# Two state matmuls of a recurrent attention loop over 128 partitions in place of 64: three become two, ten become six

## The chip, the cores and the metric

The kernel runs on one core of a Trainium2 chip. The metric is the device time of one execution in microseconds. Beside the plain runs there is one execution under the hardware profiler, and every row below comes from it.

## The reference, cut to what matters

A small network of two layers: cross attention, a quantised feed-forward, then a recurrent attention with a state of 64 values, and a mixture of experts. The change touches only the recurrent part. It has 256 steps that follow one another, for a batch of 4. In the reference, one step is

```python
def step(carry, tgt):
    s, c, alpha = carry
    f = conv(alpha, conv_w)
    e = einsum('a,bta->bt', va, tanh(enc_proj + (s @ Wa_s.T)[:, None, :] + einsum('bft,af->bta', f, Wa_f) + ba))
    alpha_new = softmax(where(mask, e, -1e30), axis=1)
    g = einsum('bt,btd->bd', alpha_new, hbatch)
    y = tanh(g @ L_gy_w.T + L_gy_b + s @ L_sy.T) @ L_yy_w.T + L_yy_b
    rec = tgt @ L_ys.T + s @ L_ss.T + g @ L_gs_w.T + L_gs_b
    ig, fg, cg, og = split(rec, 4, axis=1)
    c_next = sig(fg) * c + sig(ig) * tanh(cg)
    s_next = sig(og) * tanh(c_next)
```

The state `s` (64 values for each of 4 sequences) enters two products in the loop: `s @ Wa_s.T` inside the tanh, and `s @ L_ss.T` inside the gates.

## The kernel before, in words

Three stages follow one another. Attention and the first feed-forward take the first 445 us. Then comes the recurrent loop, 128 turns of a hardware loop with two steps in each (`l` is the step), and last the mixture of experts. In the loop each engine has its own instruction queue, worked off in order, and the engines are tied together by semaphores alone.

Float32 numbers are multiplied in 16-bit pieces. The state is kept as `sh` (its fp16 rounding) and `sl` (the rest), each of 64 partitions by 4 columns. `was2` holds the high and the low half of `Wa_s` (64 partitions, two blocks of 128 columns), `lss3` three bf16 parts of `L_ss` (64 partitions, three blocks of 256 columns).

One step of the loop, from the end of the state's update:

- VectorE (DVE) writes `sh` (L783), `s2` (L784, float32) and `sl` (L786).
- TensorE (PE) adds the state into `bank[0]`, where the encoder part already lies: three matmuls at L1200 with 64 contraction rows and 128 moving columns each, high weights times `sh`, low weights times `sh`, high weights times `sl`. The first waits for `sh`, the third for `sl`; the last raises `pre_done`.
- PE then forms `s @ L_ss.T` in `bank[6]`: ten matmuls at L1206, again 64 rows, 4 moving columns each, five for either half of the gates. The last raises `sp_done`.
- `keep_busy(n)` (L1188) is a matmul of n moving columns over 128 partitions into a bank that nobody reads. One of 384 columns follows the ten.
- ScalarE (ACT) waits for `pre_done` and takes the tanh twice: L955 in fp16 (`th_hi`), L956 in float32 (`th`).
- DVE, in its own order: L743 waits for `sp_done` and adds the input's part of the gates (`rs`); L746 waits for L956 and writes `th_lo`, the rest of the tanh; L749 takes a maximum.
- PE, in its own order: eight small matmuls at L1214 on `th_hi`, two at L1219, a `keep_busy(512)`, and L1222 on `th_lo`, which raises `et_done`.
- ACT takes the exponentials (L960, L961) once `et_done` and the maximum are there. Softmax sums, gates, the next cell and the next `sh` follow from them. Two `keep_busy(512)` are the last matmuls ahead of the next step's L1200.

Before the loop, DVE splits the weights (`in_parts` and `in_halves`, L705 to L713) while TensorE is in the second feed-forward half, and POOL (GpSimd) clears `sh` and `sl`. TensorE waits before the loop until `part_ready` is 5.

Of the kernel before, what the change touches and what calls it, by code (L numbers as in the profile page):

```python
# [7 lines left out]
ALU = mybir.AluOpType  # L8
ACT = mybir.ActivationFunctionType
F32 = mybir.dt.float32  # L10
F16 = mybir.dt.float16
BF16 = mybir.dt.bfloat16
# [4 lines left out]
P = 128  # L17
B, S, H = 4, 256, 512
# [9 lines left out]
J = 64  # L28
KW = 101
FCH = 10  # L30
TH = T // 2
# [46 lines left out]
def build(nc, a, out):  # L78
    with ExitStack() as ctx:
        def sb(name, shape, dt=F32):  # L80
            return ctx.enter_context(nc.sbuf_tensor(name, shape, dt))

        def sem(name):
            return ctx.enter_context(nc.semaphore(name))
# [34 lines left out]
        lss3 = sb("lss3", [J, 3, 256], BF16)  # L119
        lsyT = sb("lsyT", [J, J])  # L120
        wasT = sb("wasT", [J, P])
        was2 = sb("was2", [J, 2, P], F16)
# [42 lines left out]
        gat = sb("gat", [P, 8])  # L165
        rs = sb("rs", [P, 8])
        ahn = sb("ahn", [P, 8])
        sh = sb("sh", [J, B], F16)
        sl = sb("sl", [J, B], F16)
        qv = krep[:, 0, :, :].rearrange("p b t -> p (b t)").rearrange("p (i b t) -> p i b t", i=2, b=B)  # L170
        tfi = sb("tfi", [J, 8])
        xs = sb("xs", [J, 2, 12])
        ab = sb("ab", [J, 8])
        tc_sb = sb("tc_sb", [J, B])
        s2 = sb("s2", [J, 2, B])
# [30 lines left out]
        bank = [ctx.enter_context(nc.psum_tensor(f"bank{i}", [P, 512], F32)) for i in range(8)]  # L206
# [62 lines left out]
        s = {n: sem("s_" + n) for n in names}  # L269
# [115 lines left out]
        def _(pool):  # L385
# [78 lines left out]

            nc.gpsimd.memset(xs[:], 0.0)
            nc.gpsimd.memset(s2[:], 0.0).then_inc(s["s_ready"], 1)
            nc.gpsimd.memset(sh[:], 0.0).then_inc(s["sh_ready"], 1)
            nc.gpsimd.memset(sl[:], 0.0).then_inc(s["sl_ready"], 1)
            nc.gpsimd.memset(vah[:], 0.0)
            nc.gpsimd.memset(vae[:], 0.0).then_inc(s["pchain"], 1)  # L470
            pool.wait_ge(s["pchain"], 3)
# [68 lines left out]
        def _(dve):  # L540
            chain = [0]

            def link(ins):

                chain[0] += 1
                ins.then_inc(s["chain"], 1)
                dve.wait_ge(s["chain"], chain[0])
# [28 lines left out]
            def dequantise(n):  # L576

                product, integers, _, _ = weight_slice(n)
                dve.wait_ge(w_in[min(n, 8)], 16)
                dve.wait_ge(w_sc[n % 4], 16 * (n // 4 + 1))  # L580
                nc.vector.scalar_tensor_tensor(product, integers, WSCALE, product, ALU.mult, ALU.mult).then_inc(s["product_ready"], 1)
# [121 lines left out]
            def in_halves(dst, src):  # L703

                link(nc.vector.tensor_copy(dst[:, 0], src))  # L705
                nc.vector.tensor_tensor(dst[:, 1], src, dst[:, 0], ALU.subtract).then_inc(s["part_ready"], 1)

            def in_parts(dst, src):

                for j in range(2):  # L710
                    link(nc.vector.tensor_copy(dst[:, j], src))
                    link(nc.vector.tensor_tensor(src, src, dst[:, j], ALU.subtract))
                nc.vector.tensor_copy(dst[:, 2], src).then_inc(s["part_ready"], 1)  # L713
# [10 lines left out]
            dve.wait_ge(s["scale_ready"], 1)  # L724
            in_parts(lss3[:], lssT[:])
            in_halves(was2[:], wasT[:])
            dve.wait_ge(s["setup_v"], 1)
            in_halves(vae2[:], vae[:].rearrange("p h b -> p (h b)"))
            swiglu(IT0, IT0, False, context_parts())
# [4 lines left out]
            def by_half(ap):  # L734
                return ap.rearrange("p (o b) -> p o b", o=2)


            with dve.Fori(0, S // 2) as i:
                for par in range(2):
                    l = i * 2 + par  # L740

                    dve.wait_ge(s["sp_done"], l + 1)
                    nc.vector.tensor_tensor(rs[:].unsqueeze(1), bank[6][:, 0:8].unsqueeze(1), rin2[:, bass.ds(i, 1), par, :], ALU.add)  # L743

                    dve.wait_ge(s["th_full"], l + 1)
                    nc.vector.tensor_tensor(th_lo, th, th_hi, ALU.subtract).then_inc(s["th_lo_ready"], 1)  # L746

                    dve.wait_ge(s["eb_done"], l + 1)
                    nc.vector.tensor_reduce(nmx[:], bank[2][:, 0:T], AX.X, ALU.max, negate=True).then_inc(s["mx_ready"], 1)  # L749

                    dve.wait_ge(s["ex_ready"], l + 1)
                    nc.vector.tensor_tensor(el[:], ex[:, par, :], eh[:], ALU.subtract).then_inc(s["el_ready"], 1)  # L752

                    dve.wait_ge(s["sum_done"], l + 1)
                    nc.vector.reciprocal(rinv[:, par, :], bank[5][:, 8:12]).then_inc(s["rinv_ready"], 1)  # L755

                    norm = rinv[:, par:par + 1, :].broadcast_to([P, 2, B])
                    dve.wait_ge(s["rinv_ready"], l + 1)
                    dve.wait_ge(s["hg_done"], l + 1)
                    nc.vector.tensor_tensor(by_half(g1[:]), by_half(bank[4][:, 0:8]), norm, ALU.mult).then_inc(s["prod_ready"], 1)  # L760

                    def spread(h):

                        return nc.vector.tensor_tensor(qv[:, h, :, :], inv[:].unsqueeze(1).broadcast_to([P, B, TH]),  # L764
                                                       ahn[:, 4 * h:4 * h + 4].unsqueeze(2).broadcast_to([P, B, TH]), ALU.mult)


                    dve.wait_ge(s["ah_done"], l + 1)
                    nc.vector.tensor_tensor(by_half(ahn[:]), by_half(bank[7][:, 0:8]), norm, ALU.mult).then_inc(s["ahn_ready"], 1)
                    dve.wait_ge(s["prod_ready"], l + 1)  # L770
                    nc.vector.tensor_tensor(gat[:], g1[:], rs[:], ALU.add).then_inc(s["g_ready"], 1)  # L771
                    dve.wait_ge(s["ahn_ready"], l + 1)
                    spread(0).then_inc(s["q0_ready"], 1)
                    dve.wait_ge(s["kept"], l + 1)
                    spread(1).then_inc(s["q1_ready"], 1)

                    dve.wait_ge(s["tg_ready"], l + 1)
                    nc.vector.scalar_tensor_tensor(ab[:], tfi[:], 1.0, xs[:, par, 0:8], ALU.add, ALU.mult).then_inc(s["ab_ready"], 1)
                    dve.wait_ge(s["ab_ready"], l + 1)
                    nc.vector.scalar_tensor_tensor(xs[:, 1 - par, 0:4], ab[:, 0:4], 0.5, ab[:, 4:8], ALU.mult, ALU.add).then_inc(s["c_ready"], 1)  # L780

                    dve.wait_ge(s["tc_ready"], l + 1)
                    nc.vector.scalar_tensor_tensor(sh[:], xs[:, par, 8:12], 1.0, tc_sb[:], ALU.add, ALU.mult).then_inc(s["sh_ready"], 1)  # L783
                    nc.vector.scalar_tensor_tensor(s2[:, 1 - par, :], xs[:, par, 8:12], 1.0, tc_sb[:], ALU.add, ALU.mult).then_inc(s["s_ready"], 1)  # L784
                    dve.wait_ge(s["s_ready"], l + 2)
                    nc.vector.tensor_tensor(sl[:], s2[:, 1 - par, :], sh[:], ALU.subtract).then_inc(s["sl_ready"], 1)  # L786

# [211 lines left out]
        def _(pe):  # L1001
            mm = nc.tensor.matmul
# [166 lines left out]
            pe.wait_ge(s["setup_v"], 1)  # L1169
            pe.wait_ge(s["mask_ready"], 1)  # L1170
            pe.wait_ge(s["rin_ready"], 2 * B)
            pe.wait_ge(s["part_ready"], 5)
            pe.wait_ge(s["identb_ready"], 1)

            def masks():
# [17 lines left out]
            with pe.Fori(0, S // 2) as i:  # L1193
                for par in range(2):
                    l = i * 2 + par

                    state_part = [(0, sh), (1, sh), (0, sl)]
                    for j, st in state_part:
                        pe.wait_ge(s["sl_ready" if st is sl else "sh_ready"], l + 1)
                        last = mm(bank[0][:, 0:P], was2[:, j, :], st[:].unsqueeze(2).broadcast_to([J, B, TH]),  # L1200
                                  start=False, stop=(st is sl), skip_group_check=True)
                    last.then_inc(s["pre_done"], 1)

                    for gp in range(2):
                        for j, st in ((0, sh), (1, sh), (2, sh), (0, sl), (1, sl)):
                            last = mm(bank[6][:, 4 * gp:4 * gp + 4], lss3[:, j, gp * P:(gp + 1) * P], st[:],  # L1206
                                      start=(j == 0 and st is sh), stop=(j == 1 and st is sl))
                    last.then_inc(s["sp_done"], 1)

                    keep_busy(384)  # L1210
# [1 line left out]
                    for b in range(B):  # L1212
                        for h in range(2):
                            last = mm(bank[2][b * TH:(b + 1) * TH, h * TH:(h + 1) * TH], vah[:, h, :], th_hi[:, b * TH:(b + 1) * TH],  # L1214
                                      start=False, stop=True, skip_group_check=True)
# [25 lines left out]
                    for h in range(2):  # L1241
                        last = mm(bank[5][:, 8:12], onesb[:], el[:, 4 * h:4 * h + 4], start=False, stop=True, skip_group_check=True)  # L1242
# [105 lines left out]
```

## Time and profile before

| | us |
|---|---|
| median of 3 runs | 1757.52 |
| lowest and highest of them | 1752.98, 1757.66 |
| the profiled execution, its own time | 1752.67 |
| span of its instructions | 1750.9 |
| recurrent loop, 256 steps | about 445 to 1578 of the span |

| engine | busy us | share of the span |
|---|---|---|
| PE | 1652.3 | 94% |
| PE weight loads (PEld) | 960.1 | 55% |
| DVE | 926.0 | 53% |
| ACT | 526.4 | 30% |
| POOL | 385.6 | 22% |

Busy PE time includes the `keep_busy` matmuls, and the rows of matmuls overlap one another: a row runs from the start of its stream to the end of its results, and the next may start long before that end. So for PE the distance from start to start is what counts. Engine names in the rows are those of the table; `xN` merges N like instructions into one row, whose time is then from the first start to the last end. Brackets at the end of a row give the idle time before it and who ended it.

### The profile page before, as it was taken

The page shows a single profiled execution, that of the slowest core. Times are in us where ns is not written, and L with a number is a line of the kernel's source. Part 1 is how long each engine was busy: PE and PEld are TensorE (multiplying, and loading weights), DVE is VectorE, ACT ScalarE, POOL GpSimd, SP SyncE. Part 2 cuts the span into 40 slices and gives each one's busy share as a digit, 9 for nine tenths or more (in the row PEclk, how much of TensorE's full clock was granted, in tenths as well). Part 3 has the DMA queues.
Part 4 walks back from the last instruction along what each step waited for, and adds up shares of the span by engine and source line. Part 5 has one row for each costly group of instructions (what it writes and reads, how often), then busy time and mean ns, then how long its engine had stood idle before and what let it go on. Part 6 is the DMA issues. An engine that isn't in the chain of part 4 may idle for free.

```text
span 1750.9 us, 47280 instructions
## 1 busy us (share of the span) xinstructions
PE 1652.3 (94%) x17747; PEld 960.1 (55%) x17747; DVE 926.0 (53%) x4293; ACT 526.4 (30%) x2023; POOL 385.6 (22%) x1030
## 2 busy tenths in 40 slices
PE   5557999999999999999999999999999999997999
PEld 3444454544555566666666666666666666663443
DVE  5996643331455555555555555555555555553422
ACT  1442230320333333333333333333333333331211
POOL 3334321220000122222222222222222222222311
PEclk8558999999999999999999999999999999997999
DMA  8430000000300000000000000000000000000000
GB/s 323 166 106 8 1 1 0 1 1 9 123 0 0 0 0 0 0 0 0 0 0 0 0 0 0 0 0 0 0 0 0 0 0 0 0 0 1 1 25 25
DMA packets 17363, 34.51 MB, mean 20 GB/s; under 512 B 7476, under 2 KB 8675, under 8 KB 17332
## 3 DMA queue, kind: packets, MB, share of 16 engines
q1 hardware_dynamic: 17332, 34.10, 5.4%
q8 instruction: 20, 0.33, 0.1%
q14 instruction: 11, 0.09, 0.0%
HBM read 32.00 MB, written 2.10 MB: 19 GB/s over the span
## 4 chain that ended last, share of the span: by engine, by line
PE 88%; DVE 8%; issue 2%; POOL 1%; ACT 1%; SPq 1%; DMA 0%; POOLq 0%; DVEq 0%; ACTq 0%
PE bank L1188 27%; PE bank L1073 11%; PE bank L1256 10%; PE bank L1088 6%; PE bank L1232 5%; PE bank L1200 4%; PE bank L1184 4%; PE bank L1206 3%; PE bank L1214 2%; PE bank L1242 2%; PE bank L1219 2%; PE bank L1178 2%; PE bank L1054 1%; DVE xn L559 1%; DVE smax L609 1%
## 5 line engine op out<-in xcount | busy, mean ns | idle before, releaser
L1188 PE MATMUL bank<-krep,identb 128*128 128x512 f16 (+1 forms) x2048 | 604.8, 373 | 0.0
L1256 PE MATMUL bank<-krep,uh 128*128 128x128 f32 x1024 | 215.8, 323 | 0.4 <-DVE krep L764 0.4
L1256 PEld LDWEIGHTS bank<-krep,uh 128*128 128x128 f32 x1024 | 150.0, 188 | 107.8 <-DVE krep L764 91.0
L493 POOL TENSOR_TENSOR sscale<-ex,rinv 128x8 f32 x256 | 50.7, 198 | 645.5 <-DVE rinv L755 645.5
L1188 PEld LDWEIGHTS bank<-krep,identb 128*128 128x128 bf16 x2048 | 171.0, 97 | 8.1
L764 DVE TENSOR_TENSOR krep<-inv,ahn 128x128 f32<-128x128 f32 x512 | 162.3, 356 | 0.0
L1073 PE MATMUL bank<-xT,wbig 128*128 128x512 f16 x672 | 158.2, 387 | 3.6 <-DVE xT L591 3.6
L963 ACT ACTIVATE xs<-gat 64x8 f32<-64x8 f32 x256 | 53.1, 207 | 285.9 <-DVE gat L771 285.9
L743 DVE TENSOR_TENSOR rs<-bank,rin 128x8 f32<-128x8 f32 x256 | 42.7, 167 | 177.5 <-PE bank L1206 177.5
L955 ACT ACTIVATE interT<-bank 128x128 f16<-128x128 f32 x256 | 70.9, 277 | 200.7 <-PE bank L1200 200.7
L1232 PEld LDWEIGHTS bank<-eh,krep 128*128 128x128 f16 x2048 | 67.7, 96 | 102.3 <-ACT eh L960 102.3
L752 DVE TENSOR_TENSOR el<-ex,eh 128x8 f16<-128x8 f32 x256 | 43.0, 168 | 149.5 <-ACT ex L961 149.5
L1088 PE MATMUL bank<-wbig,interT 128*128 128x512 f16 x504 | 115.5, 387 | 1.4 <-POOL interT L449 1.4
L960 ACT ACTIVATE eh<-bank,nmx 128x8 f16<-128x8 f32 x256 | 68.5, 268 | 153.6 <-PE bank L1222 153.6
L1073 PEld LDWEIGHTS bank<-xT,wbig 128*128 128x128 f16 x672 | 66.9, 101 | 83.6 <-issue 14.2
L490 POOL COPY sscale<-s 64x4 f32 x256 | 45.9, 179 | 242.5 <-DVE s L784 242.5
L652 DVE SCALAR_TENSOR_TENSOR act_sb<-tanh_sb,bank 128x512 f32<-128x512 f32 x42 | 28.9, 688 | 129.6 <-ACT tanh_sb L895 129.5
L449 POOL TENSOR_TENSOR interT<-act_sb,interT 128x512 f16<-128x512 f32 x42 | 48.8, 1162 | 210.0 <-ACT interT L884 210.0
L1232 PE MATMUL bank<-eh,krep 128*128 128x4 f16 x2048 | 90.3, 166 | 0.0
L1184 PE MATMUL bank<-enc,identb 128*128 128x128 bf16 x771 | 87.7, 223 | 0.0
L1200 PEld LDWEIGHTS bank<-sh,was 64*128 64x128 f16 x512 | 28.3, 94 | 108.2 <-DVE sh L783 108.1
L755 DVE RECIPROCAL rinv<-bank 128x4 f32<-128x4 f32 x256 | 46.8, 183 | 76.1 <-PE bank L1242 76.1
(205 smaller groups left out, 3150.9 us busy)
## 6 DMA issues: line engine op xcount, KB each, us to landing
wbig<-d_gate_qT SPq DMA_DIRECT2D x4, 896.0 KB, 10.0
wbig<-d_up_qT SPq DMA_DIRECT2D x4, 896.0 KB, 20.8
wbig<-d_down_qT SPq DMA_DIRECT2D x1, 3584.0 KB, 30.6
d_out<-x_sb SPq DMA_DIRECT2D x8, 256.0 KB, 2.0
sscale<-d_gate_sT SPq DMA_DIRECT2D x2, 896.0 KB, 8.5
interT<-d_gate_sT SPq DMA_DIRECT2D x2, 896.0 KB, 14.9
sscale<-d_up_sT SPq DMA_DIRECT2D x2, 896.0 KB, 4.2
interT<-d_up_sT SPq DMA_DIRECT2D x2, 896.0 KB, 4.2
```

The source lines that it names most:

```text
L764: return nc.vector.tensor_tensor(qv[:, h, :, :], inv[:].unsqueeze(1).broadcast_to([P, B, TH]), ahn[:, 4 * h:4 * h + 4].unsqueeze(2).broadc ...
L955: nc.scalar.activation(th_hi, bank[0][:, 0:P], ACT.Tanh).then_inc(s["th_s"], 1)
L960: nc.scalar.activation(eh[:], bank[3][:, 0:8], ACT.Exp, bias=nmx[:, 0:1]).then_inc(s["eh_ready"], 1)
L963: nc.scalar.activation(xs[:, par, 4:12], gat[J:P, :], ACT.Tanh, scale=0.5)
L1073: last = mm(bk[:], w[wi][:, kt, it * P:(it + 1) * P], x[xi][:, kt, :], start=(kt == 0 and wi + xi == 0), stop=(kt == KT - 1 and xi == 1))
L1088: last = mm(bank[6 + b % 2][:], i_part[ii][:, it, b * CL:(b + 1) * CL], w[wi][:, it, :], start=(it == 0 and ii + wi == 0), stop=(it == til ...
L1184: mm(bank[0][:, 0:P], identb[:], enc3[:, j, :], start=(j == 0), stop=False, skip_group_check=True)
L1188: mm(bank[1][:, 0:n], identb[:], hg2[:, 0].rearrange("p h g -> p (h g)")[:, 0:n], start=True, stop=True)
L1200: last = mm(bank[0][:, 0:P], was2[:, j, :], st[:].unsqueeze(2).broadcast_to([J, B, TH]), start=False, stop=(st is sl), skip_group_check=True)
L1206: last = mm(bank[6][:, 4 * gp:4 * gp + 4], lss3[:, j, gp * P:(gp + 1) * P], st[:], start=(j == 0 and st is sh), stop=(j == 1 and st is sl))
L1232: ins = mm(bank[4][:, 4 * gp:4 * gp + 4], hg2[:, j, h, gp * P:(gp + 1) * P], e[:, 4 * h:4 * h + 4], start=(first and gp == 0 and j == 0 an ...
L1256: mm(bank[0][:, 0:P], uh[:, h, :], qv[:, h, :, :], start=False, stop=False, skip_group_check=True)
```

## The change

The two halves of the state are laid on the two halves of one tile: `ss` has 128 partitions, `sh` is its lower 64 and `sl` its upper 64. Two new weight tiles hold the same weights on both halves: `was_twice` (high half of `Wa_s`), `lss_twice` (first two parts of `L_ss`). One matmul over 128 partitions then gives the high weights times `sh` plus the same weights times `sl`. What has no partner with `sl` (the low half of `Wa_s`, the third part of `L_ss`) stays a matmul over 64 partitions with `sh`.

L1200: low weights times `sh` (64 rows, waits for `sh`), then `was_twice` times `ss` (128 rows, waits for `sl`). L1206: for either half of the gates one matmul over 64 rows, then two over 128. Before the loop DVE makes four more copies, and POOL clears the whole tile twice, the second time after a wait for the first.

```diff
-        sh = sb("sh", [J, B], F16)
-        sl = sb("sl", [J, B], F16)
+        ss = sb("ss", [P, B], F16)
+        sh, sl = ss[0:J, :], ss[J:P, :]
+        was_twice = sb("was_twice", [P, P], F16)
+        lss_twice = sb("lss_twice", [P, 2, 256], BF16)
...
-            nc.gpsimd.memset(sh[:], 0.0).then_inc(s["sh_ready"], 1)
-            nc.gpsimd.memset(sl[:], 0.0).then_inc(s["sl_ready"], 1)
+            nc.gpsimd.memset(ss[:], 0.0).then_inc(s["sh_ready"], 1)
+            pool.wait_ge(s["sh_ready"], 1)
+            nc.gpsimd.memset(ss[:], 0.0).then_inc(s["sl_ready"], 1)
...
             in_halves(was2[:], wasT[:])
+            dve.wait_ge(s["part_ready"], 2)
+            for half in (slice(0, J), slice(J, P)):
+                nc.vector.tensor_copy(lss_twice[half], lss3[:, 0:2, :])
+                last = nc.vector.tensor_copy(was_twice[half], was2[:, 0, :])
+            last.then_inc(s["part_ready"], 1)
...
-                    nc.vector.tensor_tensor(sl[:], s2[:, 1 - par, :], sh[:], ALU.subtract).then_inc(s["sl_ready"], 1)
+                    nc.vector.tensor_tensor(sl, s2[:, 1 - par, :], sh, ALU.subtract).then_inc(s["sl_ready"], 1)
...
-            pe.wait_ge(s["part_ready"], 5)
+            pe.wait_ge(s["part_ready"], 6)
...
-                    state_part = [(0, sh), (1, sh), (0, sl)]
-                    for j, st in state_part:
-                        pe.wait_ge(s["sl_ready" if st is sl else "sh_ready"], l + 1)
-                        last = mm(bank[0][:, 0:P], was2[:, j, :], st[:].unsqueeze(2).broadcast_to([J, B, TH]),
-                                  start=False, stop=(st is sl), skip_group_check=True)
-                    last.then_inc(s["pre_done"], 1)
+                    pe.wait_ge(s["sh_ready"], l + 1)
+                    mm(bank[0][:, 0:P], was2[:, 1, :], sh.unsqueeze(2).broadcast_to([J, B, TH]), start=False, stop=False, skip_group_check=True)
+                    pe.wait_ge(s["sl_ready"], l + 1)
+                    mm(bank[0][:, 0:P], was_twice[:], ss[:].unsqueeze(2).broadcast_to([P, B, TH]),
+                       start=False, stop=True, skip_group_check=True).then_inc(s["pre_done"], 1)
 
                     for gp in range(2):
-                        for j, st in ((0, sh), (1, sh), (2, sh), (0, sl), (1, sl)):
-                            last = mm(bank[6][:, 4 * gp:4 * gp + 4], lss3[:, j, gp * P:(gp + 1) * P], st[:],
-                                      start=(j == 0 and st is sh), stop=(j == 1 and st is sl))
+                        mm(bank[6][:, 4 * gp:4 * gp + 4], lss3[:, 2, gp * P:(gp + 1) * P], sh, start=True, stop=False)
+                        for j in range(2):
+                            last = mm(bank[6][:, 4 * gp:4 * gp + 4], lss_twice[:, j, gp * P:(gp + 1) * P], ss[:], start=False, stop=(j == 1))
                     last.then_inc(s["sp_done"], 1)
```

## Rows read from the trace of the kernel before

**Rows 1.** The page: the chain that ended last, share by engine.
```profile
PE 88%; DVE 8%; issue 2%; POOL 1%; ACT 1%; SPq 1%; DMA 0%; POOLq 0%; DVEq 0%; ACTq 0%
```

**Rows 2.** Windows, the loop: busy by engine (count), then PEclk, DMA share, GB/s.
```profile
445.00:1578.00 1133.00, 1132.56 (x15365) 687.85 (x15363) 638.21 (x3838) 381.87 (x1792) 229.44 (x850) 1.00 0.01 2
```

**Rows 3.** Timeline of one step: start us, us, engine line, operation, count.
```profile
1002.24 0.59 PE L1188 MATMUL bank<-krep,identb 128*128 128x512 f16 x2
1002.40 0.15 DVE L783 SCALAR_TENSOR_TENSOR sh<-xs,tc_sb 64x4 f16<-64x4 f32 x1 [0.27 <-ACT tc_sb L966]
1002.48 0.15 DVE L784 SCALAR_TENSOR_TENSOR s<-xs,tc_sb 64x4 f32<-64x4 f32 x1
1002.66 0.15 DVE L786 TENSOR_TENSOR sl<-s,sh 64x4 f16<-64x4 f32 x1
...
1002.77 0.28 PE L1200 MATMUL bank<-sh,was 64*128 64x128 f16 x2
...
1002.90 0.21 PE L1200 MATMUL bank<-sl,was 64*128 64x128 f16 x1
...
1002.95 0.21 PE L1206 MATMUL bank<-sh,lss 64*128 64x4 f16 x3
...
1003.15 0.19 PE L1206 MATMUL bank<-sl,lss 64*128 64x4 f16 x2
...
1003.27 0.34 PE L1188 MATMUL bank<-krep,identb 128*128 128x384 f16 x1
1003.32 0.27 ACT L956 ACTIVATE interT<-bank 128x128 f32<-128x128 f32 x1
1003.49 0.17 DVE L743 TENSOR_TENSOR rs<-bank,rin 128x8 f32<-128x8 f32 x1 [0.67 <-PE bank L1206]
...
1003.63 0.29 DVE L746 TENSOR_TENSOR interT<-interT 128x128 f16<-128x128 f32 x1
...
1003.77 0.38 PE L1188 MATMUL bank<-krep,identb 128*128 128x512 f16 x1
...
1003.99 0.17 PE L1222 MATMUL bank<-vae,interT 128*128 128x8 f16 x1
...
1004.19 0.27 ACT L960 ACTIVATE eh<-bank,nmx 128x8 f16<-128x8 f32 x1 [0.60 <-PE bank L1222]
```

**Rows 4.** Timeline of the next step, the same instructions.
```profile
1007.16 0.28 PE L1200 MATMUL bank<-sh,was 64*128 64x128 f16 x2
...
1007.30 0.23 PE L1200 MATMUL bank<-sl,was 64*128 64x128 f16 x1
...
1007.90 0.17 DVE L743 TENSOR_TENSOR rs<-bank,rin 128x8 f32<-128x8 f32 x1 [0.66 <-PE bank L1206]
...
1008.04 0.29 DVE L746 TENSOR_TENSOR interT<-interT 128x128 f16<-128x128 f32 x1
```

**Rows 5.** Timeline, matmuls of 128, 4, 6 and 128 rows in turn.
```profile
1000.66 0.17 PE L1248 MATMUL bank<-el,fwd 128*128 128x8 f16 x1
...
1000.75 0.20 PE L1178 MATMUL bank<-maskb,bsel 4*128 4x64 bf16 x1
...
1000.79 0.17 PE L1179 MATMUL bank<-etr,etl 6*128 6x8 bf16 x1
...
1000.89 0.34 PE L1184 MATMUL bank<-enc,identb 128*128 128x128 bf16 x3
```

**Rows 6.** Timeline of the loop's first step, where `sh` and `sl` are long ready.
```profile
445.02 0.34 PE L1184 MATMUL bank<-enc,identb 128*128 128x128 bf16 x3
...
445.30 0.28 PE L1200 MATMUL bank<-sh,was 64*128 64x128 f16 x2
```

**Rows 7.** Timeline ahead of the loop, DVE: splitting weights, and its next pause.
```profile
315.54 0.28 DVE L711 CAST lss<-lssT 64x256 bf16<-64x256 f32 x1
...
323.30 0.69 DVE L652 SCALAR_TENSOR_TENSOR act_sb<-tanh_sb,bank 128x512 f32<-128x512 f32 x1 [4.65 <-ACT tanh_sb L895]
```

More of the change, by code:

```diff
@@ L782, in _ @@
                     dve.wait_ge(s["tc_ready"], l + 1)
-                    nc.vector.scalar_tensor_tensor(sh[:], xs[:, par, 8:12], 1.0, tc_sb[:], ALU.add, ALU.mult).then_inc(s["sh_ready"], 1)
+                    nc.vector.scalar_tensor_tensor(sh, xs[:, par, 8:12], 1.0, tc_sb[:], ALU.add, ALU.mult).then_inc(s["sh_ready"], 1)
                     nc.vector.scalar_tensor_tensor(s2[:, 1 - par, :], xs[:, par, 8:12], 1.0, tc_sb[:], ALU.add, ALU.mult).then_inc(s["s_ready"], 1)
                     dve.wait_ge(s["s_ready"], l + 2)
-                    nc.vector.tensor_tensor(sl[:], s2[:, 1 - par, :], sh[:], ALU.subtract).then_inc(s["sl_ready"], 1)
+                    nc.vector.tensor_tensor(sl, s2[:, 1 - par, :], sh, ALU.subtract).then_inc(s["sl_ready"], 1)
             def prelude(c):
```

## Prediction

> **What bounds the kernel now.** I read the chain that ended last first. It gives PE 88% [rows 1], but PE is filled with `keep_busy` matmuls and its chain time overlaps real waits, so this share alone doesn't say that fewer matmuls make a shorter step. The second view is the windows: the loop is 1133 us of the span of 1750.9 [rows 2], and 1133 / 256 = 4.43 us a step. The granted clock there is 1.00, the 2.4 GHz level. The third view is the timeline of one step, and what the reader is to see in it is which of an instruction's conditions came last.
>
> Around the change, four such places decide. (a) The first L1200 starts at 1002.77. `sh` was finished at 1002.40 + 0.15 = 1002.55, so it isn't that. The two `keep_busy(512)` ahead start at 1002.24 and, as the pair takes 0.59 and one 0.38, 0.59 - 0.38 = 0.21 apart, at 1002.45; L1200 comes 0.32 behind the second [rows 3]. (b) The matmul on `sl` starts at 1002.90; `sl` ended at 1002.66 + 0.15 = 1002.81. In the next step it stands 0.14 behind the first L1200, more than the two streams ahead of it need (0.13 in the step before), so there it waits for `sl` alone [rows 3, 4]. (c) `th_lo` (L746) starts at 1003.63. L956 ended at 1003.32 + 0.27 = 1003.59. L743 started at 1003.49, and DVE can issue the next instruction 0.08 after a start (1002.40 to 1002.48), so L743 had cleared the way by 1003.57 [rows 3]. The tanh came last, with some 0.05 us to spare for L743. That is the whole slack of the ten small matmuls. (d) L1222 starts at 1003.99, behind `th_lo` (1003.63 + 0.29 = 1003.92) and behind the `keep_busy(512)` (1003.77 + 0.21 = 1003.98), both about equally late. ACT's exponential then names L1222 as its releaser [rows 3]. Behind it all hangs on the exponentials up to the next `sh`, so a delay of L1222 is a delay of the step.
>
> **The key price: what a matmul costs when the number of its rows changes.** The ten L1206 start from 1002.95 to the second of the pair at 1003.15, about 1003.175: nine gaps, 0.225 / 9 = 0.025 us each [rows 3]. Then the next L1188, which has 128 rows in place of 64, starts at 1003.27, 0.09 to 0.10 behind, although it waits for no semaphore [rows 3]. The same at other places. From L1248 (128 rows, 8 columns) to L1178 (4 rows) it is 0.09; from L1179 (6 rows) to L1184 (128 rows) 0.10; but from L1178 to L1179, both small, 0.04 [rows 5]. From 128 to 64 rows: at the loop's start the three L1184 take 0.34 together, and one of 128 columns 0.21 to 0.23 [rows 3, 4], so the third begins 0.11 to 0.13 behind the first, at about 445.14, and L1200 at 445.30, some 0.15 behind, with nothing to wait for [rows 6]; and place (a) above is 0.32 with a stream of 0.21. The pattern: with the same rows the next matmul starts when the stream ahead ends (0.025 at least); with other rows it starts about 0.095 us after the end of that stream. The kernel before pays this twice around the state, into the three and out of the ten. The rows fit what the Trainium skill says in "TensorEngine Tiling (Array Packing)", Key Properties: changing the tiling mode drains TensorE, and its table counts a contraction of 64 rows as a mode of its own. It gives no price; the rows do.
>
> **The change part by part, on TensorE.** The new order of rows is 128 (`keep_busy`), 64 (low weights), 128 (`was_twice`), 64, 128, 128, 64, 128, 128, then `keep_busy` with 128. That is six changes in place of two. Only matmuls are dropped that cost little: one of 128 columns (0.055 to 0.065 us) and four of 4 columns (0.025 each), 0.16 us together. I work in the step of rows 3, with the one of rows 4 in brackets.
>
> 1. Low weights times `sh`: same place behind the same `keep_busy`, 1002.77 (1007.16).
> 2. `was_twice`: behind 128 columns and a change, 0.15 by rows 6: 1002.92 (1007.31), against 1002.90 (1007.30). Its load can't be sent ahead now, so its row is 0.23 as in rows 4 and not 0.21 in the first of the two steps. `pre_done` comes 0.01 to 0.04 later. A weight load over 128 rows costs what one over 64 does as far as the rows can tell: I take no difference for the wider matmul itself.
> 3. The six small ones. Into the first: 0.15. Into its 128-row partner: 0.09. The second 128-row one: 0.04, as L1179 behind L1178, because its load too had to wait [rows 5]. Into the second half: 0.09, then 0.09 and 0.04. Sum 0.50. The last starts at 1003.42 (1007.81). Before, the last of ten started at 1003.175 (L743 less the same distance 0.315: 1007.585). So `sp_done` comes 0.245 (0.225) later, mean 0.235.
> 4. `keep_busy(384)` needs no change of rows now, 0.03 behind: 1003.45 against 1003.27, +0.18 (+0.16). Everything in PE's order behind it, the 8 and 2 small ones and `keep_busy(512)`, moves with it at the same distances, since `th_hi` was there before. So the `keep_busy(512)` ahead of L1222 leaves at +0.17 on the mean.
>
> **On VectorE.** L743 waits for `sp_done`, and what is queued behind it is L746, which PE and then ACT wait for. L743 moves from 1003.49 to 1003.735 (1007.90 to 1008.125). L746 follows by 0.08 to 0.10; I take 0.09: 1003.825 against 1003.63, +0.195 (1008.215 against 1008.04, +0.175). The spare 0.05 of place (c) is used up, and L743 becomes what comes last. `sl` is now written on other partitions than its inputs: the shown price of L786 is 0.15; no row has this form on DVE, so I take 0 with bounds of -0.01 and +0.03 (one more pause as between L784 and L786).
>
> **The path.** L1222 waits for the later of `th_lo` (+0.185 on the mean) and the `keep_busy` (+0.17). Since the two were level, I take +0.18. All that follows, up to the next `sh`, moves as a whole. POOL's copy of the state, for which a later DVE instruction waits, starts from `s2` ahead of all this and doesn't move. 256 x 0.18 = 46 us.
>
> **Outside the loop.** Four DVE copies of some 0.2 to 0.28 us, about 1 us, plus a wait for what is already in order. They stand before DVE's work for the feed-forward; its next pause there is 4.65 us [rows 7], so they cost nothing; without that cover 1 us. POOL's wait between two clears of a tiny tile stands 130 us ahead of the loop: nothing.
>
> **Sum.** 1752.67 + 46 = 1798.7 for an execution like the profiled one. That one lies 4.9 us under the median of the runs; added to the median it gives 1803.6. I forecast the middle, 1801.
>
> **Rivals.**
>
> *No price for changing rows* (ends on the other side). If the gaps of 0.09 came from something else, say from the bank or a `keep_busy` that follows, then fewer matmuls are simply fewer: the last of six small ones would start 0.11 earlier, L1222 0.01 earlier in one step (the `keep_busy` goes first, `th_lo` doesn't) and 0.03 in the other (the `sl` matmul no longer stands behind two). 256 x 0.02 = 5 us: 1748 to 1752. It decides if a change of rows costs under 0.05 us, for then L743 stays inside its slack. For it speaks that both PE and the chain look full. Against it: four places with changed rows show the gap, those of one kind don't [rows 3, 5, 6]. Chance 0.04. The Trainium skill, "TensorE: Matmul & The Clock Gate", section on the 56 ns gap, names only a floor of about 25 ns for a small matmul; the rows agree on the floor, and read alone it leads to this rival.
>
> *Only one direction costs.* If 64 to 128 costs and 128 to 64 doesn't, three of the six gaps fall away: the last small one starts at 1002.92 + 0.055 + 0.09 + 0.04 + 0.025 + 0.09 + 0.04 = 1003.26, +0.085, and L743 pushes L746 by 0.035. 256 x 0.035 = 9: 1762 to 1767. Against it: rows 6, where 128 to 64 costs 0.095 with nothing to wait for. Chance 0.04.
>
> *PE's queue alone.* If L743 doesn't hold up L746 (the 0.315 from the last small matmul to L743 could shrink), then only the `keep_busy` path counts: 0.17 or, with shorter gaps, 0.14: 1788 to 1799. Chance 0.12.
>
> *The clock falls.* PE streams fewer columns a step and pauses more, six times. In the loop the clock is 1.00 throughout [rows 2]. At the 1.2 GHz level a `keep_busy(512)` would stream 0.43 in place of 0.21; five of them stand directly ahead of real work, which gives an estimate of 5 x 0.21 = 1.05 us a step, some 2020 us. What is taken away is 144 columns a step, where the `keep_busy` matmuls alone stream 3968, and the new pauses last 0.1 us each. Chance 0.02.
>
> **How the numbers follow.** The forecast has 0.78, and its own range is that of the gap's price: 0.085 to 0.105 a change, and 0.08 to 0.14 from L743 to L746, gives 0.15 to 0.22 a step, 1791 to 1814 between the two bases. The range 1787 to 1815 takes in the PE-only rival and leaves out about 0.1 for the others and some more for the unknown. A measurement of this kernel can tell 0.3% (5 us) from no change. Faster by more: 0.02; within: 0.03; slower by more: 0.95.
>
> **What would show it.** In the profile after: a step of 4.61 us; from the low-weight matmul to `was_twice` 0.15; six changes of 0.09 to 0.15; the last small matmul 0.65 behind the first L1200 (before 0.41); L743 then L746 0.09 apart, with L746 no longer tied to L956; L1222 1.40 behind the first L1200 in place of 1.22. The forecast is wrong if the small matmuls stand 0.025 apart, or if L746 still starts 0.04 behind L956.

## The result

| | us |
|---|---|
| changed kernel, median of 4 runs | 1810.19 (1807.91 to 1813.45) |
| kernel before, median of 4 runs | 1757.59 (1752.98 to 1761.06) |
| ratio | 1.0307, 95% interval 1.0288 to 1.0327 |
| span of the profiled execution | 1806.1, before 1750.9 |

The changed kernel is 3.1% slower, by 52.6 us between the medians and 55.2 us between the spans. It lies inside the stated range, 9 us above the forecast of 1801.

**The loop carries all of it.** First the view of the line that writes `sh`, before (L783) and now (L791), then the windows of the loop now, columns as in [rows 2].

```profile
L783 DVE SCALAR_TENSOR_TENSOR sh<-xs,tc_sb x256: 153/155/156, 449.3 to 1577.9; 64x4 f16<-64x4 f32 x128
```

```profile
L791 DVE SCALAR_TENSOR_TENSOR ss<-xs,tc_sb x256: 153/154/155, 449.2 to 1634.4; 64x4 f16<-64x4 f32 x128
```

```profile
453.00:1634.00 1181.00, 1179.65 (x13974) 695.50 (x13973) 613.79 (x3812) 379.36 (x1779) 229.11 (x847) 1.00 0.00 0
```

From the first `sh` to the last a step is (1634.4 - 449.2) / 255 = 4.648 us, where it was (1577.9 - 449.3) / 255 = 4.426: +0.222, and 0.222 x 256 = 57 us. The granted clock is 1.00 in both. TensorE's matmuls fell from 17747 to 16467 by the two pages of the profile, and the time rose.

**One step of the changed kernel**, the timeline that answers to [rows 3]; L1206 and L1208 are the two state matmuls, L1212 and L1214 the six, PEld is the weight load of the second, L1196 `keep_busy`, L964 the float32 tanh, L751 `rs`, L754 `th_lo`, L1229 the former L1222, L968 the exponential.

```profile
1001.58 0.59 PE L1196 MATMUL bank<-krep,identb 128*128 128x512 f16 x2
1001.73 0.15 DVE L791 SCALAR_TENSOR_TENSOR ss<-xs,tc_sb 64x4 f16<-64x4 f32 x1 [0.27 <-ACT tc_sb L974]
...
1001.99 0.15 DVE L794 TENSOR_TENSOR ss<-s,ss 64x4 f16<-64x4 f32 x1
...
1002.10 0.23 PE L1206 MATMUL bank<-ss,was 64*128 64x128 f16 x1
...
1002.26 0.10 PEld L1208 LDWEIGHTS bank<-ss,was_twice 128*128 128x128 f16 x1
1002.26 0.23 PE L1208 MATMUL bank<-ss,was_twice 128*128 128x128 f16 x1
...
1002.42 0.17 PE L1212 MATMUL bank<-ss,lss 64*128 64x4 f16 x1
...
1002.53 0.20 PE L1214 MATMUL bank<-ss,lss_twice 128*128 128x4 f16 x2
...
1002.67 0.17 PE L1212 MATMUL bank<-ss,lss 64*128 64x4 f16 x1
1002.70 0.27 ACT L964 ACTIVATE interT<-bank 128x128 f32<-128x128 f32 x1
...
1002.77 0.20 PE L1214 MATMUL bank<-ss,lss_twice 128*128 128x4 f16 x2
...
1002.84 0.32 PE L1196 MATMUL bank<-krep,identb 128*128 128x384 f16 x1
...
1003.12 0.17 DVE L751 TENSOR_TENSOR rs<-bank,rin 128x8 f32<-128x8 f32 x1 [0.98 <-PE bank L1214]
1003.21 0.28 DVE L754 TENSOR_TENSOR interT<-interT 128x128 f16<-128x128 f32 x1
...
1003.33 0.38 PE L1196 MATMUL bank<-krep,identb 128*128 128x512 f16 x1
...
1003.55 0.18 PE L1229 MATMUL bank<-vae,interT 128*128 128x8 f16 x1
...
1003.76 0.27 ACT L968 ACTIVATE eh<-bank,nmx 128x8 f16<-128x8 f32 x1 [0.79 <-PE bank L1229]
```

Every matmul whose number of rows differs from that of the matmul ahead starts late: 1002.10 to 1002.26 and to 1002.42 (0.16 each, behind 128 columns), to 1002.53 (0.11), from the second L1214 at 1002.57 to 1002.67 (0.10), to 1002.77 (0.10 to 0.11). Where the rows don't change the distance is short: 0.03 from the last small matmul to `keep_busy`, 0.04 between the two L1214 of a pair. The last small matmul starts at 1002.81, 0.71 behind the first L1206; before it was 0.41 [rows 3]. `th_lo` stands 0.09 behind `rs` and 0.24 behind the end of the tanh (1002.97), where it had followed that end by 0.04 [rows 3]. The pause of ACT ahead of the exponential grew from 0.60 [rows 3] to 0.79.

### The profile page after: what moved, and what is told of

Same layout as the page of the kernel before. It is cut to its first block, busy times and chain, and to the rows that moved or that the text cites. A ratio compares the mean times of both kernels' runs of the same rounds, so it can differ in the third digit from the quotient of the medians.

```text
span 1806.1 us, 44724 instructions
## 1 busy us (share of the span) xinstructions
PE 1704.9 (94%) x16467; PEld 971.3 (54%) x16467; DVE 906.5 (50%) x4297; ACT 526.6 (29%) x2023; POOL 385.9 (21%) x1030
## 4 chain that ended last, share of the span: by engine, by line
PE 88%; DVE 7%; issue 2%; POOL 1%; ACT 1%; SPq 1%; DMA 0%; POOLq 0%; DVEq 0%; ACTq 0%
PE bank L1196 25%; PE bank L1081 11%; PE bank L1263 10%; PE bank L1096 6%; PE bank L1239 5%; PE bank L1192 4%; PE bank L1214 4%; PE bank L1212 3%; PE bank L1208 2%; PE bank L1221 2%; PE bank L1249 2%; PE bank L1206 2%; PE bank L1226 2%; PE bank L1186 2%; PE bank L1062 1%
## 5 line engine op out<-in xcount | busy, mean ns | idle before, releaser
L1196 PE MATMUL bank<-krep,identb 128*128 128x512 f16 (+1 forms) x2048 | 605.6, 371 | 0.0
L1196 PEld LDWEIGHTS bank<-krep,identb 128*128 128x128 bf16 x2048 | 171.2, 97 | 3.0
L751 DVE TENSOR_TENSOR rs<-bank,rin 128x8 f32<-128x8 f32 x256 | 42.6, 166 | 250.7 <-PE bank L1214 250.7
L968 ACT ACTIVATE eh<-bank,nmx 128x8 f16<-128x8 f32 x256 | 68.6, 268 | 201.9 <-PE bank L1229 201.9
L1214 PE MATMUL bank<-ss,lss_twice 128*128 128x4 f16 x1024 | 104.2, 171 | 0.0
L1212 PE MATMUL bank<-ss,lss 64*128 64x4 f16 x512 | 89.2, 174 | 0.0
```

The source lines that it names most:

```text
L968: nc.scalar.activation(eh[:], bank[3][:, 0:8], ACT.Exp, bias=nmx[:, 0:1]).then_inc(s["eh_ready"], 1)
L1196: mm(bank[1][:, 0:n], identb[:], hg2[:, 0].rearrange("p h g -> p (h g)")[:, 0:n], start=True, stop=True)
L1212: mm(bank[6][:, 4 * gp:4 * gp + 4], lss3[:, 2, gp * P:(gp + 1) * P], sh, start=True, stop=False)
L1214: last = mm(bank[6][:, 4 * gp:4 * gp + 4], lss_twice[:, j, gp * P:(gp + 1) * P], ss[:], start=False, stop=(j == 1))
```

## The experiments

The step length of each run is the distance from the first to the last write of `sh` in its profiled execution, over 255, as above. In the code J is 64 and P is 128. "Changes of rows" counts the matmuls from the first state matmul to the `keep_busy` behind the small ones that have another number of rows than the one ahead.

| label | changes of rows around the state | step us | ratio to before, 95% interval |
|---|---|---|---|
| before | 2 | 4.426 | 1 |
| changed kernel | 6 | 4.648 | 1.0307 (1.0288 to 1.0327) |
| e1_padded | 0 | 4.427 | 0.9984 (0.9974 to 0.9994) |
| e13_padded_again | 0 | 4.426 | 0.9985 (0.9972 to 0.9998) |
| e2_all_128 | 0 | 4.562 | 1.0194 (1.0177 to 1.0211) |
| e11_all_128_one_wait | 0 | 4.486 | 1.0067 (1.0045 to 1.0089) |
| e3_small_padded | 2 | 4.459 | 1.0030 (1.0010 to 1.0050) |
| e5_grouped | 4 | 4.458 | 1.0032 (1.0019 to 1.0046) |
| e6_state_pair_alone | 4 | 4.562 | 1.0202 (1.0178 to 1.0226) |
| e7_six_alone | 4 | 4.642 | 1.0306 (1.0279 to 1.0333) |
| e12_six_alone_later_wait | 4 | 4.534 | 1.0155 (1.0120 to 1.0191) |
| e4_rs_late | 6 | 4.629 | 1.0291 (1.0274 to 1.0309) |
| e9_short_filler | 6 | 4.648 | 1.0300 (1.0276 to 1.0325) |
| e10_short_filler_rs_late | 6 | 4.521 | 1.0123 (1.0094 to 1.0151) |

**Is it the wider matmul, or the change of rows?** e1_padded widens all 13 of the kernel before.

```diff
-        sh = sb("sh", [J, B], F16)
-        sl = sb("sl", [J, B], F16)
+        sh = sb("sh", [P, B], F16)
+        sl = sb("sl", [P, B], F16)
...
-            in_parts(lss3[:], lssT[:])
-            in_halves(was2[:], wasT[:])
+            nc.vector.memset(lss3[J:P], 0.0)
+            nc.vector.memset(was2[J:P], 0.0)
+            in_parts(lss3[0:J], lssT[:])
+            in_halves(was2[0:J], wasT[:])
```

> The kernel before with its three and ten matmuls, but all 13 over 128 partitions: the upper 64 of the state tiles and of the weights are zeros. Same results, same number of matmuls, no change of rows around the state. Theory (a change of rows costs a pause behind the stream ahead, about 0.09 to 0.11 us; a matmul over 128 rows is no dearer than one over 64): the distance from the last of the ten to keep_busy(384) falls from 0.09 to 0.025 us, the first L1200 comes some 0.1 us earlier behind the keep_busy, but sl and the tanh still come last, so the step loses 0 to 0.02 us: 1750 to 1758 us. Rival (the wider operands themselves cost, and the 0.22 us a step of the changed kernel come from them): 13 wider matmuls in place of five, so clearly slower than before, 1800 us or more.

Measured: 1753.04 us, ratio 0.9984. The timeline of e1_padded: two `keep_busy(512)` (L1190), the three state matmuls (L1202), the small ones (L1208) and the filler behind them.

```profile
1001.06 0.59 PE L1190 MATMUL bank<-krep,identb 128*128 128x512 f16 x2
1001.49 0.28 PE L1202 MATMUL bank<-sh,was 128*128 128x128 f16 x2
1001.68 0.23 PE L1202 MATMUL bank<-sl,was 128*128 128x128 f16 x1
1001.75 0.22 PE L1208 MATMUL bank<-sh,lss 128*128 128x4 f16 x3
...
1001.95 0.19 PE L1208 MATMUL bank<-sl,lss 128*128 128x4 f16 x2
...
1002.00 0.32 PE L1190 MATMUL bank<-krep,identb 128*128 128x384 f16 x1
```

Ten small matmuls over 128 rows take from 1001.75 to about 1001.975, as the ten over 64 did [rows 3], and the filler now follows at 0.025 instead of 0.09. The first state matmul stands 0.22 behind the second `keep_busy(512)` (1001.06 + 0.21), one stream, instead of 0.32. So width costs nothing and both pauses belong to the change of rows; the rival falls. Almost nothing is gained either: the matmul on `sl` still waits for `sl`, and `th_lo` for the tanh.

e13_padded_again is the same kernel in five rounds.

> The kernel of e1_padded once more, in five rounds, beside the others on this chip, to see if its small gain over the kernel before holds. By its timeline the step is as long as before within 0.002 us, since sl and the tanh come last in both; so the theory expects a ratio of 0.998 to 1.000, and the rival (two changes of rows less are worth what six cost) 0.985 or less.

Measured: 1753.53 us, ratio 0.9985 (0.9972 to 0.9998). The small gain of 0.15% held in both. The profiled steps don't show where it is (4.427 against 4.426), so its cause stays open.

**Which of the changes of rows cost?** In the changed kernel, e3_small_padded widens only the two small 64-row matmuls; e5_grouped leaves every width and only reorders the six.

```diff
-                        mm(bank[6][...], lss3[:, 2, gp * P:(gp + 1) * P], sh, start=True, stop=False)
+                        mm(bank[6][...], lss3[:, 2, gp * P:(gp + 1) * P], ss[:], start=True, stop=False)
```

> The changed kernel with only the two small 64-row matmuls of the six widened to 128 rows (zeros). Changes of rows around the state: two in place of six, both around the low-weight state matmul. Theory: was_twice still starts 0.16 us behind the low-weight one, so pre_done stays 0.02 to 0.05 us later than before, and the rest of the loss is gone: 0.035 x 256 = 9 us, 1766 us (1760 to 1772). Rival (the loss sits in the state pair, not in the six): stays above 1795 us.

```diff
+                    for gp in range(2):
+                        for j in range(2):
+                            mm(bank[6][...], lss_twice[:, j, ...], ss[:], start=(gp == 0 and j == 0), ...)
+                    for gp in range(2):
+                        last = mm(bank[6][...], lss3[:, 2, ...], sh, start=False, stop=True, ...)
```

> The changed kernel, same eight matmuls with the same rows each, but the six in another order: the four over 128 rows first, behind was_twice, then the two over 64. Changes of rows: four in place of six. Theory: two pauses of 0.1 us fall away and two streams stand behind a neighbour of their own kind; the last of the six ends about where the last of the ten ended before, rs is early enough, and only the 0.02 to 0.05 us of the state pair remain: 1762 to 1772 us. Rival (the total of wide matmuls or the mixing in one bank costs, whatever the order): stays near 1810 us.

Measured: 1761.28 us for e3, inside its range, and 1761.07 us for e5, one microsecond under its range. Timeline of e3_small_padded, then of e5_grouped, from the low-weight matmul to the filler:

```profile
1003.86 0.23 PE L1207 MATMUL bank<-ss,was 64*128 64x128 f16 x1
1004.02 0.23 PE L1209 MATMUL bank<-ss,was_twice 128*128 128x128 f16 x1
1004.08 0.17 PE L1213 MATMUL bank<-ss,lss 128*128 128x4 f16 x1
...
1004.19 0.19 PE L1215 MATMUL bank<-ss,lss_twice 128*128 128x4 f16 x2
1004.24 0.32 PE L1197 MATMUL bank<-krep,identb 128*128 128x384 f16 x1
```

```profile
1001.98 0.23 PE L1208 MATMUL bank<-ss,was_twice 128*128 128x128 f16 x1
1002.04 0.24 PE L1213 MATMUL bank<-ss,lss_twice 128*128 128x4 f16 x4
1002.22 0.20 PE L1215 MATMUL bank<-ss,lss 64*128 64x4 f16 x2
1002.35 0.34 PE L1196 MATMUL bank<-krep,identb 128*128 128x384 f16 x1
```

In e3 the six are 0.03 apart; in e5 the same six matmuls as in the changed kernel, in another order, leave two pauses (1002.12 to 1002.22 ahead of the 64-row ones, and 1002.26 to 1002.35 behind them). Either edit gives back 0.19 of the 0.22 us a step, e5 with exactly the same work. The 0.03 us that stay go with the state pair: 0.16 from the low-weight matmul to `was_twice` in both, and the tanh comes 0.03 later behind `sh` than in the kernel before (medians over the loop, 0.95 against 0.92), with `th_lo` right behind it.

**The two parts alone.** e6_state_pair_alone keeps the ten (and DVE writes `sl` once more, to the lower partitions); e7_six_alone keeps the three and has the six.

```diff
+                    nc.vector.tensor_tensor(sl_low[:], s2[:, 1 - par, :], sh, ALU.subtract).then_inc(s["sl_low_ready"], 1)
...
+                        for j, st in ((0, sh), (1, sh), (2, sh), (0, sl_low), (1, sl_low)):
```

> Part of the change alone: two state matmuls (64 rows, then was_twice over 128), but the ten small ones as before over 64 rows. For this DVE writes sl a second time, on the lower partitions, behind the first. Changes of rows: four. Theory: was_twice 0.16 us behind the first, the ten begin 0.16 us behind it, and keep_busy(384) starts 0.125 to 0.155 us later than before; PE's own queue then holds L1222: 0.14 x 256 = 36 us, 1785 to 1797 us. Rival (the six are the whole loss): 1758 to 1770 us.

Measured: 1792.42 us, as expected; by the medians over the loop the ten start 0.16 behind `was_twice` and the filler 0.09 behind the ten.

> The other part alone: three state matmuls over 64 rows as before, and the six of the change. sl is first written on the lower partitions for the three, then again on the upper ones for the six. Changes of rows: five in place of two. Theory: the last of the six starts 0.15 us later than the last of the ten did, keep_busy(384) 0.08 us later, th_lo 0.09 us later: 0.08 x 256 = 20 us, 1772 to 1785 us. Rival (no cost in the six, they are fewer): 1755 or less.

Measured: 1810.97 us, 26 us above the expected range. The expectation counts five changes of rows; in the order 64, 64, 64, 64, 128, 128, 64, 128, 128 behind a `keep_busy` of 128 rows there are four. The 0.15 us that it gives for the last of the six fits the four. The timeline of e7_six_alone shows what cost more (L1216 is the first of the six):

```profile
1001.48 0.15 DVE L794 SCALAR_TENSOR_TENSOR s<-xs,tc_sb 64x4 f32<-64x4 f32 x1
1001.66 0.15 DVE L796 TENSOR_TENSOR sl_low<-s,ss 64x4 f16<-64x4 f32 x1
...
1001.85 0.16 DVE L797 TENSOR_TENSOR ss<-s,ss 64x4 f16<-64x4 f32 x1
...
1001.90 0.21 PE L1210 MATMUL bank<-sl_low,was 64*128 64x128 f16 x1
...
1002.06 0.17 PE L1216 MATMUL bank<-ss,lss 64*128 64x4 f16 x1
```

The second write of `sl`, for the upper half, starts 0.19 behind the first, just after its end (1001.81), although no semaphore wait stands between them. So it ends at 1002.01, and the first of the six, without a change of rows ahead, comes 0.16 behind the matmul ahead instead of 0.06. The experiment had put a delay of its own into the queue. e12_six_alone_later_wait moves that wait behind the first small matmul, which reads only `sh`:

```diff
-                    pe.wait_ge(s["sl_ready"], l + 1)
 
                     for gp in range(2):
                         mm(bank[6][...], lss3[:, 2, gp * P:(gp + 1) * P], sh, start=True, stop=False)
+                        pe.wait_ge(s["sl_ready"], l + 1)
```

> As e7_six_alone, but the wait for the upper copy of sl stands behind the first small matmul, which doesn't need it. In e7 that wait held the six for 0.12 us, because DVE started the second write of sl only when the first had ended (0.19 us after its start, where two writes to the same partitions start 0.08 us apart). Theory: without it the six cost what their changes of rows cost: keep_busy(384) 0.10 us later than before, th_lo 0.11 to 0.12 us later: 0.11 x 256 = 28 us, 1780 to 1789 us. Rival (the wait wasn't what made e7 slower than expected): stays near 1810 us.

Measured: 1781.68 us, in the range; the step is 4.534, +0.108. So the six alone cost 0.11 and the state pair alone 0.136, in sum a little more than the 0.222 of both. e5, e6 and e12 have four changes each and cost 0.03, 0.14 and 0.11 us: the number of changes alone doesn't give the price, but where they stand does.

**No changes of rows left.** e2_all_128 widens everything in the changed kernel; its low-weight matmul then has to wait for `sl` too.

```diff
                     pe.wait_ge(s["sh_ready"], l + 1)
-                    mm(bank[0][:, 0:P], was2[:, 1, :], sh.unsqueeze(2).broadcast_to([J, B, TH]), ...)
                     pe.wait_ge(s["sl_ready"], l + 1)
+                    mm(bank[0][:, 0:P], was2[:, 1, :], ss[:].unsqueeze(2).broadcast_to([P, B, TH]), ...)
```

> The changed kernel with its two and six matmuls, but the three that stood alone over 64 rows now also over 128 (weights zero in the upper half, moving tile ss). The low-weight state matmul then reads sl's half too and must wait for sl. No change of rows is left. Theory: the six stand 0.025 us apart; one more stream of 0.06 us lies behind sl, so pre_done comes about 0.045 us later than before: 0.045 x 256 = 12 us, 1766 us (1760 to 1773). Rival (something of the twofold tile itself costs, such as sl written to other partitions than it is read from, or the two halves read at once): near the changed kernel, 1800 to 1815 us.

Measured: 1790.12 us, 24 us above the 1766 of the theory and 10 us under the rival's range: neither held. Two waits now stood in a row. The view of line L1208 (the second wait) of e2_all_128, and its timeline:

```profile
L1208 PEldq EVENT_SEMAPHORE  x197: 51/51/51, 704.3 to 1598.5; - x197
```

```profile
1000.63 0.15 DVE L796 TENSOR_TENSOR ss<-s,ss 64x4 f16<-64x4 f32 x1
...
1000.90 0.10 PEld L1209 LDWEIGHTS bank<-ss,was 128*128 128x128 f16 x1 [0.59 <-DVE ss L793]
1000.93 0.22 PE L1209 MATMUL bank<-ss,was 128*128 128x128 f16 x1
```

The load comes 0.12 behind the end of `sl` (1000.78). e11_all_128_one_wait drops the first wait.

> As e2_all_128, but with one wait ahead of the first state matmul instead of two (sl is written after sh, so the wait for sl covers both). In e2 the weight load came 0.116 us behind the end of sl instead of 0.05, and PE's queue shows an instruction of its own for the second wait, 0.05 us. Theory (the second wait in a row is what e2 lost beyond one stream): load 0.05 behind sl, pre_done 0.04 us later than in the kernel before, 10 us: 1764 to 1770 us. Rival (reading both halves at once or the padded tiles cost): stays at 1785 to 1795 us.

Measured: 1767.64 us, in the range. The load comes 0.05 to 0.06 behind `sl` in the timeline of e11_all_128_one_wait:

```profile
1001.96 0.16 DVE L796 TENSOR_TENSOR ss<-s,ss 64x4 f16<-64x4 f32 x1
...
1002.17 0.10 PEld L1208 LDWEIGHTS bank<-ss,was 128*128 128x128 f16 x1 [0.53 <-DVE ss L796]
```

So the tile with `sh` and `sl` on its halves costs nothing by itself: two and six matmuls without changes of rows are 0.7% slower than three and ten. That is about the one stream more that now stands behind `sl`: 0.060 us a step, against a stream of 0.055 to 0.065.

**Who holds L1229 in the changed kernel?** Two single cuts, then both. e4_rs_late moves the wait for `sp_done` and `rs` behind the maximum on DVE; e9_short_filler has `keep_busy(128)` for `keep_busy(384)`; e10 has both.

```diff
-                    dve.wait_ge(s["sp_done"], l + 1)
-                    nc.vector.tensor_tensor(rs[:]...)
...
                     nc.vector.tensor_reduce(nmx[:], ..., negate=True).then_inc(s["mx_ready"], 1)
+                    dve.wait_ge(s["sp_done"], l + 1)
+                    nc.vector.tensor_tensor(rs[:]...)
...
-                    keep_busy(384)
+                    keep_busy(128)
```

> The changed kernel with one DVE instruction moved: the one that waits for sp_done (rs) is placed behind th_lo and the maximum. Theory of the prediction (L746 behind rs, and PE's own queue with keep_busy ahead of L1229, are level): th_lo starts 0.2 us earlier, but L1229 still waits for the keep_busy(512) ahead of it, so the step gains only 0.01 to 0.025 us, 3 to 6 us: 1804 to 1808 us. Rival (VectorE's order alone holds the step): th_lo is back on the tanh, and the step gains 0.17 to 0.2 us, 1760 to 1768 us.

> The changed kernel with keep_busy(384) cut to keep_busy(128). PE's queue behind it moves 0.11 us forward. Theory (VectorE's order and PE's queue are level in holding L1229): th_lo is still held by rs, so the step gains at most 0.01 us: 1806 to 1813 us, same as the changed kernel. Rival (PE's queue alone holds): 0.1 x 256 = 26 us less, 1784 us.

> The changed kernel with both: rs moved behind the maximum on DVE, and keep_busy(384) cut to 128 columns. Each alone moved the time by 0.2% at most. Theory (two paths of nearly equal length hold L1229, rs on VectorE and the filler on PE): with both shortened, PE's queue is still the longer, by 0.08 us over th_lo, and L1229 ends 0.13 us earlier than in the changed kernel: 0.13 x 256 = 33 us less, 1774 to 1780 us. Rival (the pauses hold the step in some third way, such as th_hi or the maximum): no more than the two alone, 1803 to 1810 us.

Measured: 1806.83, 1809.55 and 1778.65 us, all three in their ranges. The timelines of e4_rs_late and then of e9_short_filler:

```profile
1000.75 0.27 ACT L964 ACTIVATE interT<-bank 128x128 f32<-128x128 f32 x1
...
1001.05 0.29 DVE L751 TENSOR_TENSOR interT<-interT 128x128 f16<-128x128 f32 x1 [0.86 <-ACT interT L964]
1001.36 0.38 PE L1196 MATMUL bank<-krep,identb 128*128 128x512 f16 x1
...
1001.58 0.17 PE L1229 MATMUL bank<-vae,interT 128*128 128x8 f16 x1
```

```profile
1003.93 0.17 DVE L751 TENSOR_TENSOR rs<-bank,rin 128x8 f32<-128x8 f32 x1 [0.97 <-PE bank L1214]
1004.01 0.28 DVE L754 TENSOR_TENSOR interT<-interT 128x128 f16<-128x128 f32 x1
1004.02 0.38 PE L1196 MATMUL bank<-krep,identb 128*128 128x512 f16 x1
...
1004.35 0.18 PE L1229 MATMUL bank<-vae,interT 128*128 128x8 f16 x1
```

In e4 `th_lo` is back on the tanh and ends at 1001.34, but L1229 starts at 1001.58, one stream (0.22) behind the `keep_busy(512)`. In e9 that filler is done at 1004.23, but `th_lo` ends at 1004.29 and L1229 follows 0.06 behind it. Alone the cuts give 0.019 and 0.000 us a step; together they give 0.127, 32 us.

## Why the prediction was right, and what it sized too small

- **What bounds the step.** Right: the matmul on `sl` waited for `sl` in every second step, `th_lo` waited for the tanh, and the ten small matmuls had only about 0.05 us of slack. e1 shows the other side of it: taking two pauses away there gives next to nothing.
- **The price of a change of rows.** Right that the pause goes with the change, shown by e1 (none left), e3 and e5 (fewer left). Start to start it was 0.07 to 0.11 us more than behind a matmul of the same rows and columns. By what the Trainium skill says in "TensorEngine Tiling (Array Packing)", Key Properties, a change of the mode drains TensorE; a pause in both directions fits that. That a plain matmul over 64 partitions stands in the mode of 64 rows, as the prediction has it, stays an inference: the runs show the pause and not its reason. In the timeline above the weight load of L1208 starts at 1002.26, 0.07 before the row of L1206 ends (1002.33), so it doesn't wait for the whole row. The size of the term was a bit low: behind 128 columns 0.16 and not 0.15. From 64 to 128 rows behind a small matmul it was 0.107 where I had taken 0.09 from [rows 3]; the matmul ahead of it in [rows 3] had had its load sent ahead and a row of 0.161 us, here it stands behind a pause itself and its row is 0.174. This term of the sum, from `was_twice` to the last of the six, was 0.50 and measured 0.55 (medians over the loop, for the two steps of a turn: 1.040 - 0.489 us and 1.084 - 0.533 us behind the start of `sh`). The last small matmul came 0.29 later instead of 0.235.
- **VectorE.** Right: `rs` became last and `th_lo` followed at 0.083 (0.09 taken), 0.235 later than before (0.185 forecast, the difference being the term above). `sl` on the upper half cost 0.00, as taken: L794 starts as far behind L792 as L786 behind L784 did.
- **The two paths level.** Right; e4, e9 and e10 show it. The rival that PE's queue alone holds the step is not what happened, but with the true pauses it would have given almost the same: e4, where only that path is left, is 0.019 us a step less. The time alone couldn't have told the two apart; the timelines do.
- **L1229 itself.** One small term was missing. Before, it stood one stream (0.215) behind the filler, its load had been sent ahead, and its row was 0.168. Now it stands 0.222 behind the filler and 0.06 behind the end of `th_lo`, as in e9: `th_lo`, for which its load waits, comes too late for the load to go out ahead, and the row is 0.179. L1229 comes 0.214 later than before and the exponential 0.223, against the 0.18 of the forecast.
- **The size.** The forecast was 0.18 us a step, 46 us, with bounds of 0.15 to 0.22; the profiled executions show 0.222, 57 us, at the upper bound. Of the difference of 0.04, 0.03 is that L1229 starts later than forecast, which goes back to the six small matmuls, and 0.01 is its longer row. Between the medians it was 52.6 us, nearer to the forecast than the loop itself is.
- **Outside the loop.** Right: the first write of `sh` in the loop is at 449.2 us of the span, in the kernel before at 449.3 by the same view; the four copies are hidden.
- **The rivals.** A free change of rows and one direction alone are refuted by the timeline of the changed kernel, where behind a small matmul both directions stand at 0.10 to 0.11 from start to start. The clock stayed at 1.00, the 2.4 GHz level.

## What to carry to other kernels

Look at the changes of the number of contraction rows in TensorE's order, and not only at the number of matmuls: here a small matmul costs 0.025 us, a change 0.07 to 0.11 us more, and it counts where it stands on the path that comes last. If halves are stacked to save matmuls, zero-pad the small neighbours too or group them by rows; e5 took back 0.19 of 0.22 us by order alone. Even so none of the versions with the stacked state was faster than the kernel before, since the small matmuls that they save weren't what the step waited for. And look at how many paths end level at the place that holds the step: cutting one of two gave 0 to 0.02 us, cutting both 0.13.

## What the runs showed that I had not expected

- Two waits in a row on TensorE: the second is an instruction of its own, 0.051 us in the queue, and the load came 0.12 us behind its releaser instead of 0.05. At one such place in the step, dropping it gave 0.076 us a step (e2 to e11), 22 us between the medians.
- Two VectorE instructions without a wait between them start 0.08 us apart when both write the lower partitions (the writes of `sh` and `s2`, in all runs), but 0.19 when the second writes another half than the first (e7; e6 the same the other way round). This agrees with the Trainium skill, "VectorE: DVE Perf Modes", section on two Vector instructions with no wait between them: one whose output starts in another quadrant is held until all earlier ones have finished. In the changed kernel it cost nothing, as `sl` waits for `s2` anyway.
